# Column sums of the weights as float32 matmuls on four column tiles, in one place of pair 0

## The chip, the cores and the metric

The kernel runs on one core of a Trainium2 chip. The metric is the device time of one execution in microseconds (us). Engines are named as in the profile: PE is TensorE (PEld its weight loads), DVE is VectorE, ACT is ScalarE, POOL is GpSimd, SP is SyncE, whose queue (SPq) issues nearly all DMAs here.

## The reference

A small network turns 64 condition vectors into softmax weights `att` over K = 8 kernels. Each of the 64 samples then gets its own 64 x 64 channel mixing matrix and bias, and the mixed input goes through a linear layer with a low-rank addition that is gated by rank:

```python
agg_w = einsum('bk,koi->boi', att, weight)        # [64, 64, 64]
agg_b = att @ bias_k                              # [64, 64]
h = einsum('boi,bih->boh', agg_w, x) + agg_b[:, :, None]     # x: [64, 64, 1024]
out = h @ W.T + b                                 # 1024 -> 1024
scores = h @ gate_w.T + gate_b                    # 4 ranks: 8, 16, 32, 64
r = RANKS[argmax(scores)]                         # top 1, its weight is 1
y = x + out + h @ A[:r].T @ B[:, :r].T
```

All arrays are float32.

## The kernel before, in words

The kernel swaps the two steps: with W' = [W.T | A.T | gate_w.T], 1024 x 1092, it computes Z = x W' for a tile of 128 rows (two samples) and then mixes: h W' = agg_w Z + agg_b (ones W'). The second term needs the **column sums of W'**: a row of 1092 numbers that is the same for every tile. Its last 68 columns (64 of A, 4 of the gate) are needed across all 128 partitions (`colsum`, lines 139 and 552), the other 1024 as high and low parts in rows 66 to 68 of `bt_l`, where they meet agg_b in rows 66 to 68 of `ut_h1` in the low-rank product (lines 1140 and 1141).

**Precision.** TensorE works on float32r operands, each number split in a high and a low part by ACT (high, a copy) and DVE (low, a subtraction). A product is three matmuls: high-high, low-high, high-low (`term`, line 1097).

**Tiling.** The 32 tiles go in 16 pairs. x is split into four blocks A11 to A22 of a pair (two tiles by two halves of the 1024 rows of W'), and W' into two rounds r = 0, 1 of blocks B11 to B22; a block is 512 rows by 272 (r = 0) or 274 (r = 1) columns, W[0] and W[1]. One `unit` (line 1107) is one block product: four steps of three matmuls into a bank of `p_p`. Later pairs use a sevenfold scheme with sums of blocks; pair 0 and round 0 of pairs 1 and 2 use the eight plain products. A `mix` (line 1113) is three matmuls with the mixing matrices `bd` into a bank of `p_o`, a `lora` (line 1133) two more into the same bank; DVE then adds the residual (line 840).

**Pair 0**, where the weights come in. SP loads sixteen half blocks `w_raw` (line 369, order `W_ORDER`), ACT splits off their high parts (`w_hi`, line 541) and DVE their low parts (`w_lo`, line 745). TensorE's order is written out by hand from line 1230: eight units go block by block as weights come (`first_unit(r, v, h, block)`, blocks 0 to 3 in round 0 and 4 to 7 in round 1), other units (`other_unit`) reuse blocks between them. In each of the four steps of a `first_unit` two column-sum matmuls (line 1168, `ones_r` as the stationary operand) run over the same high and low parts; they sum two blocks, on all 128 output rows, into one of the four banks `ps_sums`. ACT copies rows 0 and 64 of such a bank to `csx` (`cs_hi`, lines 549 to 557), DVE makes the low part (`cs_lo`, line 766), and SP stores three rows of each of four column ranges to `bt_l` (`sum_rows`, lines 408 to 414). POOL forms the routing bias from `colsum` (`u_bias`, line 506), which DVE's `route` (line 843) needs before TensorE may transpose (line 1129).

**Float32 matmuls** stand in the kernel already: lines 1153 to 1160 and, between the units of pair 0, lines 1206 to 1211. Line 1206 issues two matmuls with 8 contraction rows and 64 output rows each, into output rows 0 to 63 and 64 to 127; line 1208 two with 32 output rows, both into rows 0 to 31.

**The mixing weights.** Those of pair 0 are made by DVE (lines 802 and 805). Those of all pairs are made by four matmuls (`mixing_chunk`, line 1220), evicted by ACT (line 619), stored to DRAM by SP in eight DMAs (line 446) once `sum_rows` is through, and loaded for pair 1 by line 418. ACT and DVE then build `bd` (lines 587, 588, 810), and the first mixing product of pair 1 (`mix(0, 1, 0, Z11)`, line 1121) waits for that.

**Order.** Each engine works in its own order, as written, and they wait for each other by semaphores. SP's queue in pair 0: weights, B, kernel parts, `k_rows` (line 424), the first two input tiles, `g_b` (line 432), `sum_rows` 0 and 1, the bias rows (line 436), two more input tiles, `sum_rows` 2 and 3, the stores of line 446, the load of line 418.

Of the kernel before, what the change touches and what calls it, by code (L numbers as in the profile page):

```python
# [5 lines left out]
F32 = mybir.dt.float32  # L6
F32R = mybir.dt.float32r
# [4 lines left out]
P = 128  # L12
# [36 lines left out]
def adaln_ffn(nc, x, xt, layer0, layer12, b2, kernels, kernel_rows, bias_k, w0, w1, b, bt, gate_b, out):  # L49
# [14 lines left out]
    ROW_BH, ROW_BL, ROW_GH, ROW_GL, ROWS = 64, 65, 66, 68, 69  # L64
    FIRST = 2
# [16 lines left out]
    with ExitStack() as ctx:  # L82
# [52 lines left out]

        csx = sb("csx", [P, O])
        b_rows = slice(96, 96 + O // P)
        b_raw, b_h, b_l = (csx[b_rows, n * P:(n + 1) * P] for n in range(3))
        colsum = sb("colsum", [P, RE])
# [61 lines left out]
        ps_sums = (p_o[:, 2, :], p_o[:, 3, :], pc, pd)  # L201
# [5 lines left out]
        SUM_COLS = (COLS[0][Z12], COLS[0][Z11], COLS[1][Z11], COLS[1][Z12])  # L207
# [52 lines left out]
        s_cs_lo = sem("s_cs_lo")  # L260
        s_b_hi = sem("s_b_hi")
# [103 lines left out]
        def _(sp):  # L365
# [42 lines left out]
            def sum_rows(n):  # L408
                cols = SUM_COLS[n]
                sp.wait_ge(s_cs_hi, n + 1)  # L410
                for row in (ROW_GH, ROW_GL):
                    sp.dma_start(bt_l[row:row + 1, cols].bitcast(F32), csx[0:1, cols]).then_inc(s_rows[n // 2], 16)
                sp.wait_ge(s_cs_lo, n + 1)
                sp.dma_start(bt_l[ROW_GH + 1:ROW_GH + 2, cols].bitcast(F32), csx[64:65, cols]).then_inc(s_rows[n // 2], 16)
# [71 lines left out]
        def _(pool):  # L486
# [33 lines left out]
            pool.wait_ge(s_cs_hi, 2)  # L520
# [9 lines left out]
        def _(act):  # L530
# [18 lines left out]
            def cs_hi(n):  # L549
                act.wait_ge(s_cs_mm, n + 1)  # L550
                if n == 0:
                    nc.scalar.activation(colsum[:, :], ps_sums[0][:, U0:W[0]], ACT.Copy)
                cols = SUM_COLS[n]
                for row in (0, 64):
                    last = nc.scalar.activation(csx[row:row + 1, cols].bitcast(F32R),
                                                ps_sums[n][row:row + 1, 0:cols.stop - cols.start], ACT.Copy)
                last.then_inc(s_cs_hi, 1)
# [88 lines left out]
            cs_hi(0)  # L646
# [3 lines left out]
            bd_hi(0, 0, 0)  # L650
            bd_hi(0, 0, 1)
            w_hi(10)
            w_hi(11)
            act.wait_ge(s_brow_in, 16)
            nc.scalar.activation(b_h.bitcast(F32R), b_raw, ACT.Copy).then_inc(s_b_hi, 1)
            cs_hi(1)
            z_hi(0, 0, 0, Z11)
            w_hi(12)
            w_hi(13)
            z_hi(0, 0, 0, Z21)  # L660
# [4 lines left out]
            cs_hi(2)  # L665
            z_hi(0, 0, 1, Z11)
            cs_hi(3)
# [69 lines left out]
        def _(dve):  # L737
# [25 lines left out]
            def cs_lo(n):  # L763
                dve.wait_ge(s_cs_hi, n + 1)
                cols = SUM_COLS[n]
                nc.vector.tensor_tensor(csx[64:65, cols].bitcast(F32R), ps_sums[n][64:65, 0:cols.stop - cols.start],
                                        csx[64:65, cols], ALU.subtract).then_inc(s_cs_lo, 1)
# [163 lines left out]
            z_lo(0, 0, 0, Z12)  # L931
            dve.wait_ge(s_cond_mm, 4)
# [7 lines left out]
            w_lo(6)  # L940
            mixing_weights(0)
            w_lo(7)
# [4 lines left out]
            cs_lo(0)  # L947
            w_lo(8)
            w_lo(9)
            dve.wait_ge(s_b_hi, 1)  # L950
            nc.vector.tensor_tensor(b_l.bitcast(F32R), b_raw, b_h, ALU.subtract).then_inc(s_b_lo, 1)
            cs_lo(1)
            z_lo(0, 0, 0, Z11)
            w_lo(10)
            w_lo(11)
            z_lo(0, 0, 0, Z21)
            for m in range(12, 16):
                w_lo(m)
# [137 lines left out]
        def _(pe):  # L1096
# [74 lines left out]
            def first_unit(r, v, h, block, between=()):  # L1171
# [3 lines left out]
                for kk in range(KH):  # L1175
# [14 lines left out]
                    if kk < len(between):  # L1190
                        between[kk]()
# [236 lines left out]
```

## Time and profile before

| | |
|---|---|
| median of 3 runs | 456.07 us (455.82 to 456.12) |
| the profiled execution's own time | 454.03 us |
| its span in the profile | 451.9 us, 10470 instructions |
| granted TensorE clock | 1.00 of full speed |
| busy share PE / DVE / ACT / POOL | 99% / 76% / 40% / 5% |
| HBM | 40.69 MB read, 18.15 MB written |

The span is the profiled execution from its first to its last instruction; the execution's own time has some 2.1 us more around it. Matmuls overlap, so that their lengths add up to more than the time they take: the distance from start to start is what one of them costs. In a timeline row the first two numbers are the start and the length of the group in us, `x4` counts its records, and a bracket at the end gives the idle time before it and what ended that.

### The profile page before, as it was taken

The page shows a single profiled execution, that of the slowest core. Times are in us where ns is not written, and L with a number is a line of the kernel's source. Part 1 is how long each engine was busy: PE and PEld are TensorE (multiplying, and loading weights), DVE is VectorE, ACT ScalarE, POOL GpSimd, SP SyncE. Part 2 cuts the span into 40 slices and gives each one's busy share as a digit, 9 for nine tenths or more (in the row PEclk, how much of TensorE's full clock was granted, in tenths as well). Part 3 has the DMA queues.
Part 4 walks back from the last instruction along what each step waited for, and adds up shares of the span by engine and source line. Part 5 has one row for each costly group of instructions (what it writes and reads, how often), then busy time and mean ns, then how long its engine had stood idle before and what let it go on. Part 6 is the DMA issues. An engine that isn't in the chain of part 4 may idle for free.

```text
span 451.9 us, 10470 instructions
## 1 busy us (share of the span) xinstructions
PE 447.3 (99%) x3505; PEld 443.5 (98%) x3505; DVE 343.9 (76%) x888; ACT 181.8 (40%) x416; POOL 21.7 (5%) x47
## 2 busy tenths in 40 slices
PE   8999999999999999999999999999999999999997
PEld 6999999999999999999999999999999999999997
DVE  5897979998696867868687786868668586876945
ACT  6664644444252333435233343423434242343511
POOL 3020000010000000000000000000000000100000
PEclk9999999999999999999999999999999999999999
DMA  7985650804416071441607144170714407061202
GB/s 258 324 243 163 171 172 6 281 1 141 147 59 229 2 244 43 158 128 46 239 0 242 43 153 131 26 259 0 243 42 132 152 15 269 0 232 55 93 2 93
DMA packets 24060, 59.17 MB, mean 131 GB/s; under 512 B 6894, under 2 KB 8994, under 8 KB 23972
## 3 DMA queue, kind: packets, MB, share of 16 engines
q1 hardware_dynamic: 23796, 58.78, 39.7%
q8 instruction: 14, 0.23, 0.2%
q10 hardware_dynamic: 240, 0.07, 0.1%
q14 instruction: 10, 0.08, 0.1%
HBM read 40.69 MB, written 18.15 MB: 130 GB/s over the span
## 4 chain that ended last, share of the span: by engine, by line
PE 95%; DVE 2%; DMA 1%; SPq 0%; issue 0%; ACT 0%
PE p_p L1103 75%; PE p_o L1121 4%; PE p_o L1123 4%; PE p_o L1141 4%; PE p_o L1122 3%; PE p_o L1140 3%; DMA w_raw<-in_w 1%; PE p_p L1168 1%; PE p_p L1129 1%; DVE wl L745 1%; PE p_o L1168 0%; DVE aggw L805 0%; PE p_p L1220 0%; DVE prod L802 0%; DVE zl L821 0%
## 5 line engine op out<-in xcount | busy, mean ns | idle before, releaser
L1103 PE MATMUL p_p<-wh,xh 128*128 128x274 f32 (+1 forms) x880 | 256.7, 292 | 0.3 <-ACT wh L541 0.3
L1103 PE MATMUL p_p<-wh,xl 128*128 128x274 f32 (+1 forms) x880 | 253.9, 289 | 0.0
L1103 PE MATMUL p_p<-wl,xh 128*128 128x272 f32 (+1 forms) x864 | 250.3, 290 | 0.0
L1103 PEld LDWEIGHTS p_p<-wh,xh 128*128 128x128 f32 x880 | 166.2, 189 | 0.9 <-ACT wh L541 0.5
L1103 PEld LDWEIGHTS p_p<-wh,xl 128*128 128x128 f32 x880 | 166.5, 189 | 0.0
L1103 PEld LDWEIGHTS p_p<-wl,xh 128*128 128x128 f32 x864 | 162.8, 188 | 0.0
L601 ACT ACTIVATE zh<-sv 128x274 fp32r<-128x274 f32 (+1 forms) x56 | 24.2, 433 | 95.0 <-DVE sv L833 95.0
L840 DVE TENSOR_TENSOR xin<-p_o,xin 128x274 f32<-128x274 f32 (+2 forms) x128 | 51.9, 417 | 1.2 <-PE p_o L1141 0.2
L578 ACT ACTIVATE xh<-s_raw 128x512 fp32r<-128x512 f32 x60 | 36.3, 628 | 17.0 <-DVE s_raw L788 16.4
L601 ACT ACTIVATE zh<-p_p 128x272 fp32r<-128x272 f32 (+1 forms) x44 | 17.4, 397 | 60.5 <-PE p_p L1103 58.0
L795 DVE TENSOR_TENSOR xl<-s_raw,xh 128x512 fp32r<-128x512 f32 x60 | 40.9, 682 | 0.1
L821 DVE TENSOR_TENSOR zl<-sv,zh 128x274 fp32r<-128x274 f32 (+1 forms) x56 | 24.9, 444 | 19.6 <-ACT zh L601 19.3
L1123 PE MATMUL p_o<-zl,bd 128*128 128x272 f32 (+1 forms) x127 | 36.9, 291 | 0.0
L1121 PE MATMUL p_o<-zh,bd 128*128 128x272 f32 (+1 forms) x127 | 36.7, 289 | 0.1
L1122 PE MATMUL p_o<-zh,bd 128*128 128x272 f32 (+1 forms) x127 | 36.5, 287 | 0.0
L773 DVE TENSOR_TENSOR xl<-raw,xh 128x512 fp32r<-128x512 f32 x45 | 33.4, 743 | 1.4 <-ACT xh L572 0.4
L1141 PE MATMUL p_o<-bt_l,ut_h 69*128 69x274 f32 (+2 forms) x127 | 34.3, 287 | 0.0
L1140 PE MATMUL p_o<-bt_h,ut_hl 128*128 128x274 f32 (+2 forms) x127 | 34.1, 286 | 0.0
L572 ACT ACTIVATE xh<-raw 128x512 fp32r<-128x512 f32 x45 | 28.3, 628 | 11.9 <-PE p_p L1103 11.9
L821 DVE TENSOR_TENSOR zl<-p_p,zh 128x272 fp32r<-128x272 f32 (+1 forms) x44 | 19.4, 440 | 15.8 <-ACT zh L601 15.4
L833 DVE TENSOR_TENSOR sv<-p_p,sv 128x274 f32<-128x274 f32 (+1 forms) x28 | 12.4, 442 | 23.3 <-PE p_p L1103 23.3
L833 DVE TENSOR_TENSOR sv<-p_p,su 128x274 f32<-128x274 f32 (+1 forms) x56 | 24.6, 439 | 3.4 <-PE p_p L1103 1.1
(151 smaller groups left out, 508.4 us busy)
## 6 DMA issues: line engine op xcount, KB each, us to landing
xin<-in_x SPq DMA_DIRECT2D x32, 512.0 KB, 4.0
raw<-in_xt SPq DMA_DIRECT2D x30, 512.0 KB, 5.0
out<-xin SPq DMA_DIRECT2D x30, 512.0 KB, 5.7
w_raw<-in_w SPq DMA_DIRECT2D x8, 274.0 KB, 7.1
w_raw<-in_w SPq DMA_DIRECT2D x8, 272.0 KB, 5.9
g_aggw<-aggw_all SPq DMA_DIRECT2D x8, 128.0 KB, 2.4
aggw<-g_aggw SPq DMA_DIRECT2D x15, 64.0 KB, 4.9
raw<-in_xt SPq DMA_DIRECT2D x3, 256.0 KB, 5.3
```

The lines of the kernel that those rows point to most:

```text
L578: nc.scalar.activation(xh[:, n, :], s_raw[:, XL_PLACE[n], :], ACT.Copy).then_inc(s_sh, 1)
L601: nc.scalar.activation(zh[:, z_place(i, j, r, n), 0:W[r]], src, ACT.Copy).then_inc(s_zh, 1)
L795: nc.vector.tensor_tensor(xl[:, XL_PLACE[n], :], s_raw[:, XL_PLACE[n], :], xh[:, n, :].bitcast(F32), ALU.subtract).then_inc(s_sl, 1)
L821: nc.vector.tensor_tensor(zl[:, at, 0:W[r]], src[:, 0:W[r]], zh[:, at, 0:W[r]].bitcast(F32), ALU.subtract).then_inc(s_zl, 1)
L833: nc.vector.tensor_tensor(to[:, 0:W[r]], bank[:, 0:W[r]], of[:, 0:W[r]], ALU.add).then_inc(s_sum, 1)
L840: nc.vector.tensor_tensor(xin[:, slot, cols], p_o[:, OBANK[n], 0:cols.stop - cols.start], xin[:, slot, cols], ALU.add).then_inc(s_y, 1)
L1103: last = nc.tensor.matmul(o[:, 0:W[r]], a, m, start=start and p == 0, stop=stop and p == 2, skip_group_check=True)
L1121: nc.tensor.matmul(o, bd[:, t, 0, :], zh[:, at, zs], start=True, stop=False)
L1122: nc.tensor.matmul(o, bd[:, t, 1, :], zh[:, at, zs], start=False, stop=False)
L1123: nc.tensor.matmul(o, bd[:, t, 0, :], zl[:, at, zs], start=False, stop=True).then_inc(s_mix, 1)
L1140: nc.tensor.matmul(o, ut_hl[:, mine], bt_h[:, cols], start=False, stop=False, skip_group_check=True)
L1141: nc.tensor.matmul(o, ut_h1[0:ROWS, mine], bt_l[0:ROWS, cols], start=False, stop=True, skip_group_check=True).then_inc(s_lora, 1)
```

## The change

The column sums no longer come from the split parts in every `first_unit`, but from `w_raw` itself by 32 float32 matmuls in one function, `column_sums`, which TensorE runs in pair 0 between the mixes of Z22 and Z11. Their stationary operand is 32 columns of ones, and the four column ranges go to output rows 0, 32, 64 and 96 on (four column tiles of the array), all into one bank (`p_o`, bank 3). Two small matmuls of two columns fill the tiles of round 0 up to 274 columns. ACT copies the last 68 columns to one row (`cs_u`), then the whole bank as high parts; DVE makes all low parts at once. `column_sums_of_u` spreads `cs_u` over 128 partitions by one float32 matmul with one contraction row. `other_unit(0, 3, 1)` moves ahead of the mixes, and the mix of Z21 one unit back. The diff shows ACT's, DVE's and PE's parts in this order. In ACT's and DVE's orders some splits and z parts change places. SP stores the same twelve rows, those of ranges 1 and 3 (round 0) first.

```diff
-        ps_sums = (p_o[:, 2, :], p_o[:, 3, :], pc, pd)
+        ps_sums = p_o[:, 3, 0:W[1]]
+        ps_sum_u = pc[:, 0:RE]
...
+        SUM_BLOCKS = ((1, (B11, B21)), (0, (B11, B21)), (1, (B12, B22)), (0, (B12, B22)))
+        SUM_COLS = (COLS[1][Z11], COLS[0][Z11], COLS[1][Z12], COLS[0][Z12])
...
             def sum_rows(n):
...
                 for row in (ROW_GH, ROW_GL):
-                    sp.dma_start(bt_l[row:row + 1, cols].bitcast(F32), csx[0:1, cols]).then_inc(s_rows[n // 2], 16)
+                    sp.dma_start(bt_l[row:row + 1, cols].bitcast(F32), cs_h[src, wide]).then_inc(done, 16)
...
-            sum_rows(0)
+            sp.wait_ge(s_cs_hi, 1)
+            sp.wait_ge(s_cs_lo, 1)
             sum_rows(1)
+            sum_rows(3)
             sp.wait_ge(s_b_stored, 16 * 2)
...
+            sum_rows(0)
             sum_rows(2)
-            sum_rows(3)
...
-            pool.wait_ge(s_cs_hi, 2)
+            pool.wait_ge(s_colsum, 1)
...
+            def column_sums():
+                act.wait_ge(s_cs_mm, 1)
+                u_row = slice(SUM_TILE * SUM_ROWS, SUM_TILE * SUM_ROWS + 1)
+                nc.scalar.activation(cs_u, ps_sums[u_row, U0:W[0]], ACT.Copy).then_inc(s_cs_u, 1)
+                nc.scalar.activation(cs_h.bitcast(F32R), ps_sums, ACT.Copy).then_inc(s_cs_hi, 1)
+
+            def column_sums_of_u():
+                act.wait_ge(s_cs_mm, 2)
+                nc.scalar.activation(colsum[:, :], ps_sum_u, ACT.Copy).then_inc(s_colsum, 1)
...
             nc.scalar.activation(bt_h[:, :], bt_raw[:, :], ACT.Copy).then_inc(s_bt_hi, 1)
-            cs_hi(2)
+            column_sums()
+            column_sums_of_u()
             z_hi(0, 0, 1, Z11)
-            cs_hi(3)
...
+            def column_sums():
+                dve.wait_ge(s_cs_hi, 1)
+                nc.vector.tensor_tensor(cs_l.bitcast(F32R), ps_sums, cs_h, ALU.subtract).then_inc(s_cs_lo, 1)
...
+            w_lo(12)
+            column_sums()
+            for m in range(13, 16):
                 w_lo(m)
             route(0, 0)
...
+            def column_sums():
+                ones_col = ones_r[:, 0:SUM_ROWS].bitcast(F32)
+                for q, (r, _) in enumerate(SUM_BLOCKS):
+                    if W[r] < W[1]:
+                        rows = slice(q * SUM_ROWS, (q + 1) * SUM_ROWS)
+                        nc.tensor.matmul(ps_sums[rows, W[r]:], ones_col, ones_r[:, 0:W[1] - W[r]].bitcast(F32),
+                                         start=True, stop=True, skip_group_check=True)
+                for k in range(2 * KH):
+                    if k % 2 == 0:
+                        for n in (B11, B21, B12, B22)[k // KH:4:2]:
+                            pe.wait_ge(s_w_in[W_ORDER.index((1, n, k // 2 % 2))], 16)
+                    for q, (r, blocks) in enumerate(SUM_BLOCKS):
+                        rows = slice(q * SUM_ROWS, (q + 1) * SUM_ROWS)
+                        last = nc.tensor.matmul(ps_sums[rows, 0:W[r]], ones_col,
+                                                w_raw[r][:, RAW_OF[blocks[k // KH]], k % KH, :],
+                                                start=k == 0, stop=k == 2 * KH - 1, skip_group_check=True)
+                last.then_inc(s_cs_mm, 1)
+
+            def column_sums_of_u():
+                pe.wait_ge(s_cs_u, 1)
+                row = slice(SUM_TILE * SUM_ROWS, SUM_TILE * SUM_ROWS + 1)
+                nc.tensor.matmul(ps_sum_u, ones_r[row, :].bitcast(F32), cs_u, start=True, stop=True).then_inc(s_cs_mm, 1)
...
-                    column_sum(n, r, w, kk, False, opens, False)
...
-                    sums = column_sum(n, r, w, kk, True, False, closes)
...
             first_unit(0, 0, 1, 3)
+            other_unit(0, 3, 1)
             pe.wait_ge(s_aggbt, 2)
             pe.wait_ge(s_aggb, 1)
             mix(0, 0, 0, Z12)
+            mix(0, 0, 0, Z22)
+            column_sums()
+            mix(0, 0, 0, Z11)
+            column_sums_of_u()
+            first_unit(1, 0, 0, 4)
             pe.wait_ge(s_cs_lo, 1)
-            mix(0, 0, 0, Z22)
-            other_unit(0, 3, 1)
-            mix(0, 0, 0, Z11)
-            first_unit(1, 0, 0, 4)
+            mix(0, 0, 0, Z21)
             first_unit(1, 0, 1, 5)
-            pe.wait_ge(s_cs_lo, 2)
-            mix(0, 0, 0, Z21)
             first_unit(1, 1, 0, 6)
             first_unit(1, 1, 1, 7)
             pe.wait_ge(s_zl, piece(0, 0, 1, Z11))
             transpose_u(0, 0)
-            pe.wait_ge(s_cs_lo, 3)
+            pe.wait_ge(s_colsum, 1)
             other_unit(1, 2, 0)
```

DVE's order around it becomes: `w_lo(6)` ahead of the copies of the attention products, `w_lo(7)` ahead of `mixing_weights(0)`, then `bd_lo`, z of Z22, `w_lo(8)`, z of Z11, `w_lo(9)`, z of Z21, `w_lo(10)`, `w_lo(11)`, the low part of b, `w_lo(12)`. ACT's: `w_hi(10)` between the two `bd_hi`, z of Z11 and Z21 behind `w_hi(11)`, b behind `w_hi(13)`.

## Rows read from the trace of the kernel before

**Rows 1.** The page's first part: busy time by engine over the span.

```profile
PE 447.3 (99%) x3505; PEld 443.5 (98%) x3505; DVE 343.9 (76%) x888; ACT 181.8 (40%) x416; POOL 21.7 (5%) x47
```

**Rows 2.** Timeline of PE, unit 0: start us, length us, engine, line, operands.

```profile
8.97 0.39 PE L1103 MATMUL p_p<-b12l,xh 128*128 128x272 f32 x1
```

**Rows 3.** Timeline of PE, end of round 0 and start of round 1.

```profile
25.56 0.29 PE L1103 MATMUL p_p<-wl,xh 128*128 128x272 f32 x1
...
25.90 0.40 PE L1121 MATMUL p_o<-zh,bd 128*128 128x272 f32 x1
...
26.38 0.29 PE L1103 MATMUL p_p<-wh,xh 128*128 128x274 f32 x1
...
31.32 0.29 PE L1168 MATMUL p_p<-wl,ones_r 128*128 128x274 f32 x1
```

**Rows 4.** Timeline of PE: a float32 matmul, and the first matmul behind small tiles.

```profile
2.88 0.64 PE L1153 MATMUL p_o<-cw 128*128 128x64 f32 x2
...
16.79 0.39 PE L1103 MATMUL p_p<-wh,xh 128*128 128x272 f32 x1
```

**Rows 5.** Timeline of VectorE, GpSimd and ScalarE, 14 to 31 us.

```profile
14.87 0.21 DVE L928 COPY attt<-p_o 8x64 f32<-8x64 f32 x1
...
24.70 0.47 POOL L509 TENSOR_TENSOR bias<-colsum,aggb 128x136 f32<-128x136 f32 x1 [19.87 <-ACT csx L555]
...
27.47 1.05 ACT L664 ACTIVATE bt_h<-bt_raw 128x1024 fp32r<-128x1024 f32 x1
...
30.17 0.29 DVE L847 TENSOR_TENSOR u<-p_o,ubias 128x136 f32<-128x136 f32 x1
```

**Rows 6.** Timeline of PE cut off at 16.006, 16.08, 16.24 and 16.375 us.

```profile
16.00 0.24 PE L1206 MATMUL p_o<-attt,bk 8*64 8x32 f32 x2
...
16.00 0.30 PE L1206 MATMUL p_o<-attt,bk 8*64 8x32 f32 x3
...
16.23 0.24 PE L1208 MATMUL p_o<-bk,attt 8*32 8x64 f32 x1
...
16.23 0.35 PE L1208 MATMUL p_o<-bk,attt 8*32 8x64 f32 x3
```

**Rows 7.** DMA queue, weights: issues in time, and landing of one line.

```profile
10.30 3.92 SPq L369 DMA_DIRECT2D w_raw<-in_w  x8
...
DMA to landing us min/median/max: 3.8/6.5/9.8
```

**Rows 8.** Timeline of the DMA queue and of PE, 30 to 49 us.

```profile
30.51 1.68 SPq L412 DMA_DIRECT2D bt_l<-csx  x2
...
36.75 0.24 SPq L436 DMA_DIRECT2D bt_l<-g_b  x1
...
40.65 0.29 PE L1140 MATMUL p_o<-bt_h,ut_hl 128*128 128x272 f32 x1
...
41.60 5.03 SPq L446 DMA_DIRECT2D g_aggw<-aggw_all  x8
...
48.47 0.40 SPq L418 DMA_DIRECT2D aggw<-g_aggw  x1
```

**Rows 9.** Timeline of pair 1 up to its first mixing product, all engines.

```profile
51.87 0.26 ACT L587 ACTIVATE bd<-aggw 64x64 fp32r<-64x64 f32 x1 [2.92 <-DMA aggw<-g_aggw]
...
52.73 0.93 DVE L810 TENSOR_TENSOR bd<-aggw,bd 64x64 fp32r<-64x64 f32 x4
...
53.95 0.29 PE L1103 MATMUL p_p<-wl,xh 128*128 128x272 f32 x1
...
54.19 0.40 PE L1121 MATMUL p_o<-zh,bd 128*128 128x272 f32 x1
```

**Rows 10.** DMA in 40 slices from 48.4 to 52 us, and its queues.

```profile
DMA  0000000000002699310000000000000000000069
...
GB/s 0 0 0 0 0 0 0 0 0 0 0 0 68 148 222 336 66 26 0 0 0 0 0 0 0 0 9 9 9 9 11 0 0 0 0 0 0 0 91 273
...
q8 instruction: 1, 0.02, 1.7%
```

More of the change, by code:

```diff
@@ L138, in adaln_ffn @@
         b_raw, b_h, b_l = (csx[b_rows, n * P:(n + 1) * P] for n in range(3))
+        cs_h, cs_l = (csx[:, 3 * P + n * W[1]:3 * P + (n + 1) * W[1]] for n in range(2))
+        cs_u = csx[SUM_TILE * SUM_ROWS:SUM_TILE * SUM_ROWS + 1, O - RE:O]
         colsum = sb("colsum", [P, RE])
@@ L946, in _ @@
             bd_lo(0, 0, 1)
-            cs_lo(0)
             w_lo(8)
+            z_lo(0, 0, 0, Z11)
             w_lo(9)
+            z_lo(0, 0, 0, Z21)
+            w_lo(10)
+            w_lo(11)
             dve.wait_ge(s_b_hi, 1)
             nc.vector.tensor_tensor(b_l.bitcast(F32R), b_raw, b_h, ALU.subtract).then_inc(s_b_lo, 1)
[L952 to L957, printed above, removed]
+            w_lo(12)
+            column_sums()
+            for m in range(13, 16):
                 w_lo(m)
             route(0, 0)
-            cs_lo(2)
             z_lo(0, 0, 1, Z11)
@@ L967, in _ @@
             t_sum(1, R11, R12, R11)
-            cs_lo(3)
             z_lo(0, 0, 1, Z22)
@@ L1164, in _, with first_unit @@
                      (pc, A11, B12), (pc, A12, B22), (pd, A21, B11), (pd, A22, B21))
-            def column_sum(n, r, w, kk, lo, start, stop):
-                m = (w_lo_place if lo else w_hi_place)(r, w)[:, kk, :]
-                return nc.tensor.matmul(ps_sums[n][:, 0:W[r]], ones_r[:, :], m, start=start, stop=stop,
-                                        skip_group_check=True)
-            def first_unit(r, v, h, block, between=()):
-                n = block // 2
+            def column_sums():
[19 more added lines that the diff above has]
+                nc.tensor.matmul(ps_sum_u, ones_r[row, :].bitcast(F32), cs_u, start=True, stop=True).then_inc(s_cs_mm, 1)
+            def first_unit(r, v, h, block):
                 o, a, w = TERMS[2 * v + h]
@@ L1182, in first_unit @@
                         pe.wait_ge(s_al, 1)
-                    opens, closes = h == 0 and kk == 0, h == 1 and kk == KH - 1
-                    term(o, a, r, w, kk, opens, False, (0, 1))
-                    column_sum(n, r, w, kk, False, opens, False)
+                    term(o, a, r, w, kk, h == 0 and kk == 0, False, (0, 1))
                     if kk % 2 == 0:
                         pe.wait_ge(s_wl, at + 1)
-                    done = term(o, a, r, w, kk, False, closes, (2,))
-                    sums = column_sum(n, r, w, kk, True, False, closes)
-                    if kk < len(between):
-                        between[kk]()
+                    done = term(o, a, r, w, kk, False, h == 1 and kk == KH - 1, (2,))
                 if h == 1:
                     done.then_inc(s_z, 1)
-                    sums.then_inc(s_cs_mm, 1)
             def attention_rows():
```

42 lines of the change are left out of this document (13 added, 29 removed).

## The prediction

> **What bounds the kernel now.** I read the page first, then the timeline of each engine over the first 55 us, then the waits of the DMA queue. TensorE is busy for 99% of the span [rows 1]: a TensorE instruction taken away is worth its pitch, as long as nothing else ends later than TensorE would then arrive. The change lies wholly in pair 0; from pair 1 on the same instructions run in the same order. What matters is the lead or lag with which TensorE comes to pair 1, and whether something that the change doesn't move holds it there.
>
> Three places already show such holders. In the first unit TensorE waits for weights: its last wait ends at 8.97 [rows 2]. The attention products, at 16.00, need a VectorE copy that ends at 14.87 + 0.21 = 15.08 [rows 5, 6]. And in pair 1 the first mixing product (line 1121) starts at 54.19, 0.24 us after the matmul before it instead of the usual 0.127: it waited for the end of a chain that comes through the DMA queue [rows 9].
>
> **What is removed.** 64 column-sum matmuls (line 1168): eight units of four steps, two each, 32 in each round. The 40 matmuls from 26.38 to 31.32 give a pitch of 4.94 / 39 = 0.127 us [rows 3], so each round sheds 4.05 us, 8.1 us gross. ScalarE and VectorE lose their one-row copies and subtractions (eight and four) and gain one full copy and one full subtraction. Both are relieved, so I cost this at nothing: where one of them is waited for, the work ahead of it is counted below.
>
> **What is added.** 32 float32 matmuls of 272 or 274 columns on four column tiles, two fillers of two columns, and one float32 matmul of 68 columns. A float32 matmul leaves two records. The two matmuls of line 1208 share a tile; cut short after the first and after the third of their four records, they last 0.24 and 0.35 us, so a record of 64 columns takes 0.055, or 0.86 ns a column [rows 6]. For 274 columns that is 0.235 us. Each tile has eight matmuls, 16 records: side by side the four take 16 x 0.235 = 3.8 us, one after the other 64 x 0.235 = 15.0. These are the two ends. Which? The matmuls of line 1206 go to two column tiles (output rows 0 to 63 and 64 to 127). By 16.006 two records run already, and only by 16.08 a third [rows 6]. On one tile, records stand 0.05 apart at least, so the two early ones are of different tiles, and the second matmul did not wait for the first one's second record. I take 3.8 us, the end that this row is nearest to. That four tiles of 128 rows do what two tiles of eight rows do is the inference in it.
>
> The Trainium skill (TensorE: Matmul & The Clock Gate, section "Measured speedup vs the span model") puts three column tiles at 2.38 times one. By that alone, as an estimate, the 3.8 us would be 3.8 x 3 / 2.38 = 4.8. No run here shows three or four tiles, and the forecast would stay the same, since the lead that is left would still be held at pair 1.
>
> Going from the whole array to tiles and back costs about 0.1 us each way (the matmul at 16.79 lasts 0.39 where others last 0.29 [rows 3, 4]) and one latency between: 0.3 us. The 68-column matmul with its changes of tile is bounded by 2 x 68 x 0.86 ns = 0.12 us below and by the 0.64 of line 1153 above [rows 4]; I take 0.5, nearer the upper row, because both load 128 columns of weights.
>
> **The path through pair 0.** (a) Units 0 and 1 lose 16 matmuls, 2.0 us, but TensorE waits. Behind 8.97 only three of the removed ones remain, so unit 0 is left 0.4 us sooner. By then 16 matmuls and the waits bring TensorE to the attention products at about 14.6, and there it waits for the copy at 15.08, whose chain on VectorE (splitting weights and activations as they land) does not move. 16.00 becomes 15.1: lead 0.9. (b) Units 2 and 3: 16 x 0.127 = 2.0, lead 2.9. (c) The column sums: 3.8 + 0.3 = 4.1. They need all weights: the last is issued by 10.30 + 3.92 = 14.2, and none lands over 9.8 us after its issue, so by 24.0; it is wanted in step 7 of 8, which begins 6 x 0.47 = 2.8 us into a stretch that starts near 22.7 [rows 7]. No wait. Then a mix, whose wait of 0.2 (from 25.56 + 0.127 to 25.90 [rows 3]) goes; then the copy of 68 columns on ScalarE. It stands behind bt_h, which ends now at 27.47 + 1.05 = 28.5 and, with the mixes 3 us sooner and nothing between, would end at about 27.1 [rows 5]. The copy takes about 0.25 (a piece of 64 columns takes 0.26 [rows 9]), so TensorE waits about 0.2, then 0.5 for the matmul. Lead 2.9 - 4.1 + 0.2 - 0.2 - 0.5 = -1.7. (d) Units 4 to 7: 4.05. Lead 2.35: LoRA, at 40.65 now, would start at 38.3 [rows 8].
>
> What stands beside it and stays covered: the routing needs colsum by way of POOL, whose first product starts at 24.70 now and would start at about 28.3; two steps of 0.5 later, 29.3, VectorE is still 0.9 us short of its routing at 30.17 [rows 5]. Without that cover the routing slips by what is missing, and TensorE transposes only at 34.5. The mix of Z21 waits for cs_lo, there at 28.2, and comes at 29.5. No DMA is added or taken, and the queue comes to its first sum rows at 30.51 [rows 8], when both halves exist.
>
> **Where the lead is held.** The queue issues the bias rows at 36.75, then without a break two input tiles and six sum rows, and from 41.60 eight stores of mixing weights for 5.03 us, waits for them, and issues the load at 48.47 [rows 8]. ScalarE gets that at 51.87 [rows 9]. None of these times depends on TensorE, unless it is late: the evictions to be stored are there 2.35 us sooner and wait. From 51.87 ScalarE's four pieces of 0.26, VectorE's bd_lo (now from 52.73) and z_lo lead to 54.19 [rows 9]. VectorE was in other work until 52.73; freed sooner, it lets the chain end 0.26 sooner, 53.93. TensorE would arrive at 54.08 - 2.35 = 51.7. If the load stays, 2.2 of the 2.35 us are lost there.
>
> But the load had a tail: a slice is 0.09 us, so nearly all traffic is over by 50.1, a trickle follows from 50.7 to 51.2, and in the same stretch stands one instruction fetch [rows 10]. With its bulk alone it lands near 50.35, 1.5 us sooner: gain 1.8. The fetch follows TensorE's instruction stream, so with the lead it would come some 3 us sooner, near 46.7, among the eight stores. They could then end 0.9 us later for it: 0.26 + 1.5 - 0.9 = 0.9. So 0.3, 0.9 and 1.8 are the bounds; I take 1.05, between the last two and nearer the first of these.
>
> **Numbers.** The profiled execution took 454.03 us for a span of 451.9, 2.04 below the median of 456.07; the gain is subtracted from the median: 455.0. A measurement of this kernel can tell about 0.2%, 0.9 us, from no change.
>
> **The rivals.** 1. Four tiles together, but the load's tail stays: gain 0.26, 455.8. The queue is the holder, which speaks for it; the fetch should move, which speaks against. Chance 0.33.
>
> 2. Records start strictly in the program's order, so that the second record of one tile keeps the next tile's first back until it can start itself. Then only neighbours overlap: 33 x 0.235 = 7.7 us instead of 3.8. LoRA comes at 42.2 instead of 40.65, nothing takes that up, and the end is 1.55 later: 457.6, slower. This decides as soon as the sums take over 3.8 + 2.35 = 6.2 us. Against it: two records by 16.006 [rows 6]. Chance 0.12.
>
> The Trainium skill (TensorE: Matmul & The Clock Gate, section "The mechanism") states this order: matmuls start and end strictly as in the program. By that rule rival 2 happens; the records of line 1206 in this trace disagree with it.
>
> 3. No overlap at all, four streams of 128 rows sharing one way into the array: 15.0 us, 11.2 more than assumed, 8.9 slower: 465.0. The same rows speak against it; for it, that none shows 128 rows. Chance 0.08.
>
> 4. My forecast, the load's tail moved or gone: gain 0.9 to 1.8, up to 2.35 if the gate opens altogether. Chance 0.47.
>
> **How the numbers follow.** Faster by over 0.2% is case 4 but for its edge: 0.45. Within 0.2% is rival 1 with that edge: 0.35. Slower are rivals 2 and 3: 0.2. The range leaves out rival 3 and the best tenth of case 4: 454.0 to 457.7.
>
> **What would show it.** Right: the column sums in one stretch from about 22.7 to 26.7, records of four tiles starting within 0.05 us of each other; a TensorE wait of 0.4 before line 1206's matmul and of 0.2 before the 68 columns; LoRA at 38.3; stores still from 41.6; and a wait of 1 to 2 us before the first mixing product of pair 1. Wrong: the stretch takes over 6 us; TensorE waits for colsum or cs_lo; or no wait stands at pair 1, and the whole 2.35 arrives.

## The result, and the profile after

| | before | after |
|---|---|---|
| median | 456.09 us (18 runs, 454.25 to 457.67) | 453.47 us (18 runs, 451.39 to 457.3) |
| profiled execution | 454.03 us | 452.71 us |
| its span | 451.9 us | 450.7 us |

The ratio is 0.9954, with a 95% interval of 0.9932 to 0.9976: 2.1 us less, between 1.1 and 3.1 (the two medians are 2.6 us apart). The forecast was 455.0 us with a range of 454.0 to 457.7; the sign was right, the size was missed, by 0.5 us beyond the low end. The two profiled executions differ by 1.32 us only, near the 1.05 that the sum gave. The work below is about that difference: what the sum got right, and why medians moved otherwise.

The page's first part after the change (against [rows 1], TensorE is busy for 3 us less):

```profile
PE 444.3 (99%) x3511; PEld 438.2 (97%) x3511; DVE 342.6 (76%) x885; ACT 179.7 (40%) x410; POOL 23.8 (5%) x47
```

The timeline of TensorE after the change, from the attention products to LoRA (columns: start us, length us, engine, line, operands, count, and in brackets the idle time before it). Lines have moved: 1107 is the products' line 1103, 1125 to 1127 are the mix, 1144 is line 1140, 1222 is line 1206; 1176 are the two-column fillers, 1184 the column sums, 1192 is the 68-column matmul.

```profile
15.25 0.30 PE L1222 MATMUL p_o<-attt,bk 8*64 8x32 f32 x4
...
22.82 0.28 PE L1127 MATMUL p_o<-zl,bd 128*128 128x272 f32 x1
23.04 0.20 PE L1176 MATMUL p_o<-ones_r 128*32 128x2 f32 x2
23.05 0.43 PE L1184 MATMUL p_o<-w_raw,ones_r 128*32 128x274 f32 x2
23.09 0.18 PE L1176 MATMUL p_o<-ones_r 128*32 128x2 f32 x2
23.12 3.84 PE L1184 MATMUL p_o<-w_raw,ones_r 128*32 128x272 f32 x62
26.89 0.40 PE L1125 MATMUL p_o<-zh,bd 128*128 128x272 f32 x1
...
27.52 0.43 PE L1192 MATMUL p_p<-csx,ones_r 1*128 1x68 f32 x2
27.88 0.40 PE L1107 MATMUL p_p<-wh,xh 128*128 128x274 f32 x1
...
38.18 0.28 PE L1144 MATMUL p_o<-bt_h,ut_hl 128*128 128x272 f32 x1
```

The attention products stand at 15.25 for a predicted 15.1, the column sums fill 23.05 to 26.89, the first unit of round 1 starts at 27.88, and LoRA at 38.18, for a predicted 38.3: a lead of 40.65 - 38.18 = 2.47 us [rows 8]. The same timeline cut off at 23.60 and at 23.84 us shows how the column sums run:

```profile
23.05 0.93 PE L1184 MATMUL p_o<-w_raw,ones_r 128*32 128x274 f32 x12
...
23.05 1.16 PE L1184 MATMUL p_o<-w_raw,ones_r 128*32 128x274 f32 x16
```

Four more records start in 0.23 us, which is the time that one record alone takes (0.235 was the sum's figure). So four column tiles with 128 rows each run side by side. They also leave the program's order: the column ranges have 274, 272, 274 and 272 columns on tiles 0 to 3, and the two records of 274 columns start at 23.05, before any of 272 columns (23.12). The matmul of tile 2 has passed that of tile 1, whose tile was still busy with the filler.

Then the DMA queue, 36 to 49 us:

```profile
36.01 0.23 SPq L446 DMA_DIRECT2D bt_l<-g_b  x1
...
40.80 6.09 SPq L456 DMA_DIRECT2D g_aggw<-aggw_all  x8
48.76 0.40 SPq L426 DMA_DIRECT2D aggw<-g_aggw  x1
```

and what waits for the load, on ScalarE, VectorE and TensorE:

```profile
50.81 0.26 ACT L597 ACTIVATE bd<-aggw 64x64 fp32r<-64x64 f32 x1 [4.31 <-DMA aggw<-g_aggw]
...
51.36 1.00 DVE L816 TENSOR_TENSOR bd<-aggw,bd 64x64 fp32r<-64x64 f32 x4 [1.01 <-ACT bd L598]
...
52.39 0.44 DVE L827 TENSOR_TENSOR zl<-p_p,zh 128x272 fp32r<-128x272 f32 x1
...
52.88 0.39 PE L1125 MATMUL p_o<-zh,bd 128*128 128x272 f32 x1 [1.10 <-DVE zl L827]
```

The queue starts its eight stores 0.8 us sooner than before (40.80 for 41.60), spends 6.09 us on them instead of 5.03, and issues the load 0.3 later. The load then needs 50.81 - 48.76 = 2.05 us until ScalarE has it, where it needed 51.87 - 48.47 = 3.40 [rows 8, 9]: its tail is gone, and the stores have become longer. Pair 1's first mixing product comes at 52.88 for 54.19, 1.31 us sooner, behind a wait of 1.10 us. The span is 1.2 us shorter. A lead of 2.47 us arrived, and 1.2 of it were lost here. That the stores start 0.8 us sooner is not the change's doing: the queue has waited for the kernel parts to land in DRAM (5.5 us, 5.6 before), and its next issue comes at 24.79 for 25.92, though the last store of the parts was issued at the same time (16.41 and 16.47). Two more profiles of the changed kernel have 25.41 (e8 below) and 25.73 (e4) there, and one of a kernel without the change 24.96 (e2). This is the queue's phase in one execution.

### The profile page after: what moved, and what is told of

Its sections match the earlier page's. It is cut to its first block, busy times and chain, and to the rows that moved or that the text cites. A ratio compares the mean times of both kernels' runs of the same rounds, so it can differ in the third digit from the quotient of the medians.

```text
span 450.7 us, 10478 instructions
## 1 busy us (share of the span) xinstructions
PE 444.3 (99%) x3511; PEld 438.2 (97%) x3511; DVE 342.6 (76%) x885; ACT 179.7 (40%) x410; POOL 23.8 (5%) x47
## 4 chain that ended last, share of the span: by engine, by line
PE 93%; DMA 2%; DVE 2%; SPq 1%; ACT 1%; issue 0%; ACTq 0%
PE p_p L1107 74%; PE p_o L1125 4%; PE p_o L1127 3%; PE p_o L1126 3%; PE p_o L1145 3%; PE p_o L1144 3%; DMA raw<-in_xt 1%; SPq L456 1%; PE p_o L1184 1%; PE p_p L1133 1%; DMA g_aggw<-aggw_all 1%; DVE wl L753 1%; DMA aggw<-g_aggw 0%; ACT aggw_all L629 0%; SPq L378 0%
```

## The experiments

Theory: TensorE's sum is right, and what is lost of the lead is lost to SP's queue, whose phase differs from execution to execution. Rivals: the column sums cost more in most executions than in the profiled one; the queue does not matter, and the gain comes from elsewhere. The first rival has nothing for it: in three profiles of the unedited change the sums take 3.85 us each time. Kernels of one group ran beside the kernel before on the same chip: 455.32 us for the first four (28 runs), 455.28 for the next four (23), 455.64 for the last four (29).

### 1. The queue shortened, in both kernels, and four tiles made one

In the changed kernel, the two input tiles that stand behind the bias rows go behind the load of pair 1's mixing weights:

```diff
-            for t in range(2, 4):
-                sp.dma_start(xin[:, t, :], x_t[t]).then_inc(s_x_in[t], 16)
             sum_rows(0)
             sum_rows(2)
...
             mixing_weights(0, 1)
+            for t in range(2, 4):
+                sp.dma_start(xin[:, t, :], x_t[t]).then_inc(s_x_in[t], 16)
```

> The changed kernel, but SP issues the two input tiles of pair 1 only behind the load of pair 1's mixing weights, so that sum rows, stores and load come sooner. If the queue holds pair 1 (the theory): stores from about 39.9 instead of 40.8, the load landed by about 49.3 instead of 50.8, no TensorE wait before the first mixing product of pair 1, and the time 1.1 us under the changed kernel's, about 3.4 under the kernel before by the medians on record. If the wait is of the one profiled execution only and other executions have none: the time is the changed kernel's, within 0.3 us. If the later input tiles are wanted sooner than they land: a new wait and a longer time.

Measured: 452.58 us (11 runs), ratio 0.993 (0.9905 to 0.9955). That is 2.6 us under the unedited change beside it (e4 below). In its profile the stores start at 39.28 and the wait has nearly gone:

```profile
51.71 0.39 PE L1125 MATMUL p_o<-zh,bd 128*128 128x272 f32 x1 [0.38 <-DVE zl L827]
```

The same edit in the kernel before, as a control:

> The kernel before with the same order of the queue. If TensorE and the queue are level in the kernel before, as its profile shows (0.1 us of wait), this gains 0.1 us at most: ratio 1.000. If most executions of the kernel before are held by the queue for longer than the profiled one, which would explain why the medians moved by 2.6 us where the profiled executions moved by 1.3, this gains 1 us or more: ratio 0.998 or less.

Measured: 455.25 us (12 runs), ratio 0.9989 (0.9969 to 1.0008). No gain from the queue's order alone can be told from nothing. In its profile the queue comes to the stores sooner, but then waits 1.8 us and starts them at 41.55, as before: the evictions that it stores come behind TensorE.

The column sums all on one tile (and the fillers made to write the whole bank):

```diff
-                    if W[r] < W[1]:
+                    for c in range(0, W[1], P):
                         rows = slice(q * SUM_ROWS, (q + 1) * SUM_ROWS)
-                        nc.tensor.matmul(ps_sums[rows, W[r]:], ones_col, ones_r[:, 0:W[1] - W[r]].bitcast(F32),
+                        nc.tensor.matmul(ps_sums[rows, c:min(c + P, W[1])], ones_col, ones_r[:, 0:min(P, W[1] - c)].bitcast(F32),
...
-                        rows = slice(q * SUM_ROWS, (q + 1) * SUM_ROWS)
+                        rows = slice(0, SUM_ROWS)
                         last = nc.tensor.matmul(ps_sums[rows, 0:W[r]], ones_col,
```

> The changed kernel with all 32 float32 matmuls on one column tile (output rows 0 to 31), so the four ranges are summed into one another and the sums in the output are left wrong; the fillers write the other rows, in twelve small float32 matmuls. If the four tiles run side by side, one tile takes 64 records x 0.235 = 15.0 us for what took 3.85, and the time is some 10 us over the changed kernel's (11.2 less the 1.1 of wait in pair 1 that it uses up). If the stretch took 3.85 us for another reason (a float32 record costs less than 0.235 us), one tile takes clearly less than 15.

Measured: 463.31 us (2 runs), ratio 1.0165 (1.0109 to 1.0221). TensorE's timeline:

```profile
24.24 14.65 PE L1184 MATMUL p_o<-w_raw,ones_r 128*32 128x274 f32 x63
38.83 0.39 PE L1125 MATMUL p_o<-zh,bd 128*128 128x272 f32 x1
```

A record takes 0.23 us here too, but now one after the other: the price of rival 3, 15.0 us, is real when no tiles overlap. The stretch is 11 us longer and the larger fillers take another 0.9; of these 11.9 us 10.4 arrive in the profiled span (461.1 for 450.7), and pair 1's wait of 1.10 us is gone. By medians it is 8.1 us over the unedited change beside it (e4). The change stands on the four tiles.

The changed kernel once more, nothing edited:

> The changed kernel once more, unedited. It gives a second profile and more runs beside the other three. If the wait in pair 1 is usual, this profile has it again, 0.8 to 1.5 us, and TensorE's LoRA starts 2.3 to 2.5 us ahead of the kernel before's. If it was chance, the wait is absent or its length is unlike 1.1 us. Ratio 0.993 to 0.998 either way.

Measured: 455.22 us (12 runs, 452.17 to 456.54), ratio 0.9986 (0.996 to 1.0013): in this group there is no gain to be seen. Its profile (455.04 us) shows a late queue and a longer wait:

```profile
28.78 1.50 SPq L437 DMA_DIRECT2D xin<-in_x  x2
...
38.30 0.23 SPq L446 DMA_DIRECT2D bt_l<-g_b  x1
...
51.18 0.40 SPq L426 DMA_DIRECT2D aggw<-g_aggw  x1
```

```profile
39.86 0.36 PE L1144 MATMUL p_o<-bt_h,ut_hl 128*128 128x272 f32 x1 [1.45 <-issue]
...
55.26 0.39 PE L1125 MATMUL p_o<-zh,bd 128*128 128x272 f32 x1 [2.10 <-DVE zl L827]
```

The bias rows are issued 2.3 us later than in the first profile. LoRA waits 1.45 us; the profile names no releaser ("issue"), but the semaphore in the kernel counts the bias rows, which are the last DMA before it. Pair 1 waits 2.10 us, and its first mixing product comes 1.07 us later than before the change. Of the lead nothing is left.

Where the 2.3 us come from can be read off the queue. It waits twice for rows that make a round trip through DRAM: the kernel parts land 0.9 us later (its next issue at 25.73 for 24.79), and the two rows of b make it wait 2.9 us for 1.8. The two input tiles between take 1.50 us of issue for 0.83, as an instruction fetch starts at 29.0, in the middle of them. Some 0.4 us are won back at the first sum rows.

### 2. Rows first, fewer column sums, another order

All four input tiles out of the way: 0 and 1 behind the bias rows, 2 and 3 behind the load.

```diff
-            for t in range(2):
-                sp.dma_start(xin[:, t, :], x_t[t]).then_inc(s_x_in[t], 16)
             sp.wait_ge(s_b_lo, 1)
...
-            for t in range(2, 4):
+            for t in range(2):
                 sp.dma_start(xin[:, t, :], x_t[t]).then_inc(s_x_in[t], 16)
...
             mixing_weights(0, 1)
+            for t in range(2, 4):
+                sp.dma_start(xin[:, t, :], x_t[t]).then_inc(s_x_in[t], 16)
```

> The changed kernel with both pairs of input tiles behind what TensorE waits for: in SP's queue the first two behind the bias rows, the next two behind the load of pair 1's mixing weights. If the lead of 2.4 us is lost only to the queue, nothing is left to lose it to: the bias rows landed by about 34 instead of 36.9 to 39.8, no wait before LoRA and at most 0.4 before pair 1's first mixing product, whatever the queue's phase, so a time at or 0.3 us under e1's, 0.992 to 0.994 of the kernel before, and a narrower spread of its runs. If the input tiles come too late for the residual (wanted at about 39): a new wait behind it, and a time no better than the changed kernel's.

Measured: 452.17 us (6 runs, 451.64 to 452.57), ratio 0.9932 (0.9905 to 0.9959). No wait of TensorE stands in its timeline between 20 and 70 us:

```profile
34.30 0.33 SPq L444 DMA_DIRECT2D bt_l<-g_b  x1
...
39.60 5.04 SPq L454 DMA_DIRECT2D g_aggw<-aggw_all  x8
48.02 0.39 SPq L426 DMA_DIRECT2D aggw<-g_aggw  x1
```

Only the first of the eight steps of the column sums (128 of 1024 rows are summed):

```diff
-                for k in range(2 * KH):
+                for k in range(1):
...
-                                                start=k == 0, stop=k == 2 * KH - 1, skip_group_check=True)
+                                                start=True, stop=True, skip_group_check=True)
```

> The changed kernel with one step of the eight in the column sums (the sums then run over 128 of the 1024 rows): 28 of 32 float32 matmuls and 3.3 us of TensorE left out, everything else in place. If the queue holds pair 1, the 3.3 us only lengthen the waits before LoRA and before the first mixing product of pair 1: the time is within 0.5 us of the changed kernel's run beside it. If TensorE itself is the bound there, the time is 3.3 us less (ratio to the kernel before 0.988 to 0.99).

Measured: 453.79 us (12 runs), ratio 0.9961 (0.994 to 0.9983), level with the unedited change. The 3.1 us (3.3 were expected) were lost, but not where expected:

```profile
27.83 0.43 PE L1192 MATMUL p_p<-csx,ones_r 1*128 1x68 f32 x2 [3.13 <-ACT csx L562]
...
36.30 0.38 PE L1133 MATMUL p_p<-ident,usplit 128*128 128x128 f32 x2
```

The 68-column matmul waits for ScalarE's copy, which stands behind the copy of bt_h: it comes at 27.83 though the sums are through 3.1 us sooner. And the wait has a second price. The same kernel's windows (start and end, width, busy time of five engines, then granted clock, DMA share, GB/s):

```profile
26.00:28.00 2.00, 0.17 (x2) 0.18 (x2) 1.28 (x3) 1.95 (x5) 0.00 (x0) 1.00 0.22 69
28.00:30.00 2.00, 2.00 (x14) 1.93 (x15) 1.77 (x3) 0.42 (x2) 1.22 (x2) 0.86 0.58 94
30.00:32.00 2.00, 2.00 (x11) 2.00 (x10) 1.93 (x9) 0.00 (x0) 1.27 (x2) 0.50 0.91 147
32.00:34.00 2.00, 2.00 (x15) 2.00 (x14) 0.88 (x6) 0.40 (x1) 0.89 (x2) 0.79 0.88 131
```

After 3.13 us of waiting TensorE is granted 1.2 GHz instead of 2.4 for a while, and the transposes come 8.47 us behind the 68-column matmul, where the unedited change needs 34.47 - 27.52 = 6.95. All twelve executions have a mean clock of 0.992 to 0.996. So this run is no test of the queue; it shows that shorter sums buy nothing here.

The two loops exchanged, all eight matmuls of one tile before the next tile's:

```diff
-                for k in range(2 * KH):
...
-                    for q, (r, blocks) in enumerate(SUM_BLOCKS):
-                        rows = slice(q * SUM_ROWS, (q + 1) * SUM_ROWS)
+                for m in range(8, 16):
+                    pe.wait_ge(s_w_in[m], 16)
+                for q, (r, blocks) in enumerate(SUM_BLOCKS):
+                    rows = slice(q * SUM_ROWS, (q + 1) * SUM_ROWS)
+                    for k in range(2 * KH):
```

> The changed kernel with the two loops of the column sums exchanged: all eight matmuls of one tile, then those of the next. If a matmul for a free tile may pass any number that wait for a busy one, the stretch stays at 3.8 to 4 us (and starts at about 23.6, when the last weights are there). If only a few may be passed, tiles overlap at their ends only and the stretch takes 10 to 15 us, the time then 5 to 10 us over the changed kernel's.

Measured: 461.36 us (4 runs), ratio 1.0155 (1.0112 to 1.0199).

```profile
24.73 12.22 PE L1183 MATMUL p_o<-w_raw,ones_r 128*32 128x274 f32 x64 [1.05 <-DMA w_raw<-in_w]
```

12.22 us, between 3.85 and 14.8: few waiting matmuls can be passed. The records' starts show how few: at each of the three changes of tile the last four records of the old tile run beside the first four of the new (27.50 to 28.22 is the first such stretch), and all others stand alone, 0.23 us apart: 64 - 3 x 4 = 52 steps of 0.23 make 12.0 us. In strict order only one record would overlap at each change, 61 steps or 14.0 us. That is rival 2 of the prediction in a weaker form: it doesn't strike the order in which the change issues, and it would strike the other.

The unedited change a third time:

> The changed kernel once more beside e5 to e7: a third profile and a third ratio. By the queue theory its LoRA starts at the later of about 38.2 and the landing of the bias rows, its first mixing product of pair 1 about 2.1 us after the landing of the mixing weights, and its time follows from the second of these; over executions the ratio lies between 0.9954 and 0.9986, the two measured so far.

Measured: 453.55 us (12 runs), ratio 0.9963 (0.994 to 0.9985); in its profile pair 1 waits 1.68 us.

### 3. A known delay, with and without the late queue

Twelve idle repeats of the first product of a unit, between the transposes and LoRA (the sum starts anew each time), put into the change and into the version with the rows first:

```diff
+            def again(times, r, v, h):
+                o, a, w = TERMS[2 * v + h]
+                for _ in range(times):
+                    term(o, a, r, w, 0, True, False, (0,))
...
             pe.wait_ge(s_colsum, 1)
+            again(12, 1, 2, 0)
             other_unit(1, 2, 0)
```

> The changed kernel with twelve more float32r matmuls of 274 columns in pair 0, just behind the transposes and before the LoRA: the first product of other_unit(1, 2, 0) is issued thirteen times, each starting the sum anew, so the result stays. At a pitch of 0.127 us that is 1.52 us of TensorE work in the lead. Theory (part of the lead is lost in the wait for the mixing weights of pair 1): the wait before pair 1's first mixing product was 1.10, 2.10 and 1.68 us in the three profiled executions; it shrinks by 1.5 us and only the rest arrives, so against the unedited change the median rises by 0.2 to 0.7 us, not by 1.5. LoRA near 39.7 to 40.3, mix wait 0 to 0.6. Rival (nothing holds the lead in most executions, the profiled ones are exceptions): the median rises by 1.5 us, to 455 or more.

> The same twelve matmuls in the version with the bias rows first. There TensorE did not wait before pair 1's first mixing product, so both theories expect nearly all of the 1.52 us to arrive: 1.3 to 1.6 us above rows_first (453.5 to 453.8). If the theory is right, this delay is dearer here than in the changed kernel by 0.8 us or more. If it costs the same in both, no queue holds the lead.

And, as a second control, the kernel before with its rows first; then the rows-first version again.

> The kernel before, with the two input tiles behind the bias rows and the next two behind the load of pair 1's mixing weights, as in rows_first. Its profiled wait at pair 1 was 0.11 us. Theory: at most 0.1 to 0.5 us are won (span 451.4 to 452.2, where the runs of before had a median span of 452.5 or 452.6), since without the lead TensorE comes about when the weights do; the spread of its runs narrows, because the executions in which the queue is late are gone. The time outside the span, 2.0 to 3.7 us in before and 2.0 to 2.15 in all kernels with the change, should stay as in before if it goes with the program and not with the queue. Rival (the queue order alone is what helps, and the column sums nothing): 452 to 453 here too.

> The version with the bias rows first once more, beside the other three, with more runs: 451.6 to 452.7, median 452.2, spread small; no wait over 0.4 us before pair 1's first mixing product.

Each execution's span is recorded, so the spans can be pooled over groups:

| kernel | runs | median us | median span | time outside the span |
|---|---|---|---|---|
| before (all three groups) | 80 | 455.49 | 452.5 | 2.96 |
| before, tiles behind the load (e2) | 12 | 455.25 | 452.15 | 3.12 |
| before, rows first (e11) | 12 | 455.35 | 452.45 | 2.96 |
| the change (three times) | 42 | 453.68 | 451.6 | 2.10 |
| the change, delayed (e9) | 12 | 453.74 | 451.7 | 2.01 |
| rows first (e5, e12) | 12 | 452.35 | 450.3 | 2.11 |
| rows first, delayed (e10) | 12 | 453.42 | 451.4 | 2.02 |

The median of the last column hides two sorts of executions. Before the change 34 of 80 executions have 2.0 to 2.3 us outside the span, the other 46 have 2.8 to 4.6, and none lies between; their spans are alike (medians 452.55 and 452.45), so that the second sort is 1.2 us dearer. The queue edits leave it as it is (16 of 24 executions of e2 and e11 are of the second sort). All 107 executions of kernels with the column tiles have 2.0 to 2.2.

The 1.52 us of delay cost 0.1 us of span in the change and 1.1 with the rows first (e9: 453.74 us, ratio 0.9969; e10: 453.42, 0.9953). Both are less than forecast, and both comparisons cross groups: e9 has no unedited change beside it, and against e12, which ran beside it, e10 is 0.5 us longer by medians and 0.9 by ratios. The ratios say the same as the pool: 0.9969 lies among the three of the unedited change (0.9954 to 0.9986), 0.9953 is 0.002 above both of the rows first (0.9932, 0.9933). The two profiles agree, with a wait in the one (e9) and none in the other (e10), whose product comes 1.51 us behind the 52.21 of e5:

```profile
53.71 0.40 PE L1125 MATMUL p_o<-zh,bd 128*128 128x272 f32 x1 [1.01 <-DVE zl L827]
```

```profile
53.72 0.39 PE L1125 MATMUL p_o<-zh,bd 128*128 128x272 f32 x1
```

With standard deviations of 1.5 and 1.2 us for the spans of the change and of e9, and 0.7 and 0.8 for the other two, the first difference is known to about 0.9 us and the second to 0.6. It points the way the theory says, and isn't proof by itself. The controls stay where before is, 455.35 for e11 (ratio 0.9993, 0.9976 to 1.001): the rival that the order of the queue alone is what helps is out.

The rows-first version measured 452.96 us this time (6 runs, ratio 0.9933, 0.9907 to 0.9959), 0.8 above the first time and above its forecast of at most 452.7. Three of its six runs have a mean clock of 0.996, the profiled one among them. Its TensorE waits and its windows show why:

```profile
PE p_p L1107 <- DVE a21l L898: 0.9, 1, 0.9
PE p_p L1107 <- ACT wh L551: 0.6, 1, 0.6
PE p_p L1107 <- DVE b12l L753: 0.5, 2, 0.2
```

```profile
10.00:12.00 2.00, 1.52 (x9) 1.52 (x10) 1.98 (x4) 1.27 (x3) 0.00 (x0) 0.78 1.07 379
12.00:14.00 2.00, 2.00 (x10) 2.00 (x10) 1.97 (x10) 1.35 (x3) 0.00 (x0) 0.50 1.04 287
14.00:16.00 2.00, 2.00 (x14) 1.74 (x14) 1.72 (x5) 1.50 (x4) 0.00 (x0) 0.87 1.06 364
```

Four waits of 2.0 us in all, between 6.4 and 10.5 us, for weights and activations that are still landing (DMA share 1.07), and then the lower clock. From 11.3 to 14.4 us a matmul takes 0.227 us instead of 0.127; some 14 of them make 1.4 us. Its LoRA comes at 40.06, 1.4 us behind that of e5, and the span is 1.3 us longer: with the rows first, TensorE's time goes through nearly one for one in these two profiles.

A lower clock is more frequent with the change. Of 80 executions of before 5 have a mean clock under 0.998, of 42 of the change 12; the median of these is 455.86 us, that of the other thirty 453.47. The three groups differ widely in it: 5 of 18, 7 of 12 (e4) and 0 of 12 (e8). The column sums that are gone from units 0 and 1 were work that TensorE had while it waited for weights, and the longer waits at LoRA and pair 1 are another possible place: a mean doesn't tell where the clock fell, and only e12's profile shows it, in the first units.

## Why the prediction was wrong in size

**(a) Removed, units 0 and 1**: the products at 15.25 for 15.1, lead 0.75 instead of 0.9. One wait was not foreseen: 0.94 us for the low part of A21 at 9.82, as unit 0 is over sooner. In the profiled execution it hid behind the wait for VectorE's copy, as the text said of the rest. In e12 it doesn't end there: with the other waits it was followed by the lower clock. The sum has no term for that.

**(b), (c), (d) The column sums and round 1**: right within 0.2 us from the end of the sums on (26.89 for 26.7); they begin at 23.05 for 22.7. The stretch took 3.85 us for 3.8 and some switching, the 68-column matmul is followed by unit 4 at 27.88, LoRA stands 0.12 us from its forecast. The cover of the routing was thinner than the forecast 0.9 us: GpSimd's two steps took 0.88 and 0.84 us instead of 0.5 each, were through at 30.19, and VectorE routed at 30.71. Taking the end of the bounds that the nearest row pointed to, two records of line 1206 at work together by 16.006 [rows 6], was right: e3 shows the other end, 14.8 us. Rivals 2 and 3 are refuted for this order. The Trainium skill (TensorE: Matmul & The Clock Gate, section "The mechanism") has matmuls start strictly in program order. This trace disagrees, with tile 2 at 23.05 and tile 1 at 23.12; e7 shows that the freedom is small. The 4.8 us that the prediction estimated from the Trainium skill's figure for three tiles are 0.95 too long.

**Where the lead is held**: the place, the chain and its parts were right. The stores had 1.06 us more (0.9 was set for the fetch of instructions that moves among them, without a row for that figure; a fetch stands at 45.3, 4.5 us sooner than before for a forecast 3, and the one issue beside it takes 1.65 us), the load's tail went (1.35; 1.5 forecast), VectorE was free (0.26 forecast, and its bd_lo now starts with the data). Only that the stores would still start at 41.6 was wrong, they start 0.8 sooner. A gain of 1.05 was taken, and 1.31 came, at this place, in this execution. That is luck in part: without the 0.8, the queue's phase in this execution, the same terms give 0.25 + 1.35 - 1.06 = 0.54.

**The step that failed** is in the numbers: "2.04 below the median of 456.07; the gain is subtracted from the median". That holds only if the median of the changed kernel stands as far above its profiled execution as that of before stands above its own. It doesn't: 453.47 - 452.71 = 0.76 us for 2.04. These 1.28 us, and 0.27 by which the profiled executions are further apart than the forecast 1.05, are the 1.5 us from 455.0 to 453.5. Three things went unseen in the sum; the first is most of the 1.28, the other two work against it.

1. *Time outside the span.* The profiled execution of before had 2.1 us of it, so it was one of the cheaper sort, and the median of before is 2.96; with the change the profiled execution has 2.0 and the median is 2.10. That is 0.83 - 0.09 = 0.74 us of the 1.28. The medians of the spans stand equally far above the profiled ones, 0.6 us (452.5 over 451.9) and 0.65 (451.35 over 450.7), and explain none of it. The rest, some 0.6 us, is that the 18 runs of before in this comparison have a median of 456.09 where the 80 later ones have 455.49; their spans are not recorded. Why the change does away with the dearer sort was not found: the profile shows nothing outside the span.
2. *The queue's phase.* In three profiled executions of the change the bias rows are issued at 36.0, 37.2 and 38.3, and pair 1 waits 1.10, 1.68 and 2.10 us. The gain is what the queue leaves over, so it differs from execution to execution: the spans reach from 449.3 to 455.2 us, with a standard deviation of 1.54 where before has 1.07. A lead that is held at a gate turns the spread of the gate into the spread of the result.
3. *The clock*, above: 12 executions of 42, some 2.4 us dearer at the median, part of which may be the late queue that comes with them.

Subtracted from 455.0, 0.74 for the first and 0.27 for the profiled executions make 454.0, the low end of the range. 2 and 3 make executions of the change longer; they can explain why the three comparisons of the same kernel gave 0.9954, 0.9986 and 0.9963 (2.6, 0.1 and 1.7 us by medians). The mean of these ratios is 0.9968, 1.5 us; the recorded 2.1 to 2.6 lies on the favourable side of that. The pooled medians of the table are 1.8 us apart, but the 18 runs of before that belong to the first comparison are not among its 80. The bounds of the gain (0.26 to 1.8) were made for one mechanism; the range should have had room for the median standing elsewhere above the profiled execution, at least the 2.04 us that it stood above in the kernel before.

What stays open: the two sorts of time outside the span; why rows take so unequally long to land in DRAM (over all profiles the queue waits 4.3 to 7.7 us for the kernel parts); and why before, whose TensorE waits 0.11 us at pair 1, spreads as it does.

The best version is the change with the rows first: 452.35 us over 12 runs, 1.3 under the change and 3.1 under before (3.1 and 2.7 beside the kernel before of its own group). With it the lead of 2.47 us arrives nearly whole (span 450.3 for 452.5). Moving two tiles only (e1) gives the same ratio, 0.993, so the runs don't tell what the other two add.

## What to carry to other kernels

Before a gain is subtracted, ask what it runs into: here the whole of it was right on TensorE, and half of it went to a queue whose order cost nothing that could be measured as long as TensorE was late. So after a gain on the bound engine, read the next wait, and reorder the queue that ends it: input tiles moved out of its way were worth 1.3 us more, beside about 1.5 of the change itself. Independent small matmuls shared the array where neighbours in the program lay on different column tiles (3.85 us); the same matmuls in the other loop order took three times as long (12.2). And of one profiled execution take the span's difference, but not its distance from the median: look first whether the time outside the span comes in two sorts, and of which one the profiled execution is.

## What was unexpected of the hardware

- Matmuls on four column tiles start out of the program's order and run side by side: 64 records in 3.85 us; 14.8 on one tile; 12.2 where eight in a row are on the same one, with four records of overlap at each change of tile.
- After waits of 2.0 us in all within 4 us (e12), and after one of 3.13 (e6), the granted clock was 0.50 for some 3 us, at a price of 1.4 and 1.5 us. It stayed at 1.00 after waits of 1.10, 1.68 and 2.10 us before pair 1, and after 1.5 us of waits in the first units of e8.
- A fetch of instructions holds up the issue on SP's queue beside which it starts. (It is taken for TensorE's: in eight profiles with the change it starts 5.4 to 7.3 us behind the first LoRA matmul.) In the change one issue of a store takes 1.65 us instead of 0.6 (fetch at 45.3). In six profiles with the fetch among the eight stores these take 5.81 to 6.41 us, in eight with the fetch outside them 5.03 to 5.05. It isn't saved there, though: in four of these eight (e1, e5, e7, e12) the fetch falls into the wait for the stores to land, which then takes 2.8 to 3.3 us instead of 1.4 to 1.8.
- A DMA of one row costs SP's queue 0.55 to 0.8 us of issue, more than an input tile's 0.42: the twelve sum rows of the changed kernel take 8.0 us of it.
